# Expert up products with the rows held and the weights moving, GELU before the turn, and row loads issued ahead of the stores

## What is computed

```
logits = h2 @ gate_w + gate_b
wts, sel = top_k(logits, 2);  wts = softmax(wts)
for e in range(8):
    he = gelu(h2 @ w1[e] + b1[e], approximate=False)      # 192 -> 768
    res = res + cw[:, e:e + 1] * (he @ w2[e] + b2[e])     # 768 -> 192
```

## Time and profile before

| | before |
|---|---|
| median of 3 runs | 1596.52 us (1596.47 to 1605.81) |
| the profiled execution | 1584.23 us, its span 1582.5 us |
| mean granted TensorE clock in it | 0.816 |
| stage of the 39 tiles: first up product to last down product | 762.2 to 969.7 us |
| PE, VectorE, ScalarE busy in the span | 79%, 49%, 30% |

### The profile page before, as it was taken

One profiled execution on the slowest core, in us unless ns is written; L12 is line 12 of the kernel. 1 busy time (PEld: TensorE's weight loads), 2 busy tenths in 40 slices (PEclk: granted clock), 3 DMA queues, 4 the chain that ended last, 5 costly groups with the idle time before them and its releaser, 6 DMA issues.

```text
span 1582.5 us, 44760 instructions
## 1 busy us (share of the span) xinstructions
PE 1256.1 (79%) x19426; PEld 978.1 (62%) x19426; DVE 774.9 (49%) x2068; ACT 471.5 (30%) x1022; POOL 238.7 (15%) x248
## 2 busy tenths in 40 slices
PE   5999999987999999973799995174888989875151
PEld 2666666664767777762577773174788888864131
DVE  2133333334555634344233333552577777755876
ACT  1233333323433433233233331042133333223040
POOL 3100000143100000007100003505333333000000
PEclk8599999988988969555799998585888879855565
DMA  9000000213100000013111111100000000000001
GB/s 317 11 22 22 22 22 22 66 47 90 47 2 2 2 2 2 2 46 111 46 36 40 38 38 50 51 0 2 3 4 4 4 3 4 4 2 1 0 0 40
DMA packets 28797, 48.47 MB, mean 31 GB/s; under 512 B 3632, under 2 KB 21696, under 8 KB 28352
## 3 DMA queue, kind: packets, MB, share of 16 engines
q1 hardware_dynamic: 25536, 39.33, 8.1%
q0 software_dynamic: 3072, 6.30, 1.3%
HBM read 33.20 MB, written 12.41 MB: 29 GB/s over the span
## 4 chain that ended last, share of the span: by engine, by line
PE 64%; DVE 17%; POOL 11%; ACT 5%; issue 3%; DMA 1%; POOLq 0%; ACTq 0%; DVEq 0%
PE ps L1023 9%; PE ps L719 8%; PE ps L1135 6%; PE ps L847 4%; PE ps L1038 4%; PE ps L784 3%; POOL big L655 3%; PE ps L725 3%; POOL big L659 3%; PE ps L872 2%; PE ps L909 2%; PE ps L739 2%; POOL rows_dram L634 2%; PE ps L767 2%; PE ps L1183 2%
## 5 line engine op out<-in xcount | busy, mean ns | idle before, releaser
L1135 PE MATMUL ps<-big 128*128 128x32 bf16 x7680 | 217.8, 181 | 52.4 <-DVE big L1918 25.4
L1135 PEld LDWEIGHTS ps<-big 128*128 128x128 bf16 x7680 | 207.2, 99 | 63.8 <-DVE big L1918 29.6
L719 PE MATMUL ps<-big,consts 97*96 97x512 f32 (+1 forms) x256 | 136.3, 660 | 13.7 <-DVE consts L1544 13.7
L1023 PE MATMUL ps<-big 128*128 128x128 bf16 x1170 | 142.0, 219 | 1.1 <-DVE big L1834 0.5
L1023 PEld LDWEIGHTS ps<-big 128*128 x1170 | 112.0, 96 | 27.6 <-issue 2.9
L1841 DVE TENSOR_TENSOR big<-big 128x512 bf16<-128x512 f32 x78 | 41.5, 558 | 104.5 <-ACT big L1448 104.2
L1906 DVE TENSOR_REDUCE big<-ps 128x24 f32<-128x48 f32 x160 | 32.8, 205 | 116.7 <-PE ps L1135 115.7
L1447 ACT ACTIVATE big<-ps 128x512 bf16<-128x512 f32 x78 | 38.2, 490 | 163.6 <-issue 129.8
L719 PEld LDWEIGHTS ps<-big,consts 97*96 97x96 f32 (+1 forms) x256 | 39.7, 174 | 69.3 <-issue 61.8
L655 POOL TENSOR_SCALAR_AFFINE_SELECT big<-big 128x1536 f32<-128x1536 f32 (+1 forms) x32 | 48.7, 1547 | 222.0 <-ACT big L1485 222.0
L1662 DVE TENSOR_REDUCE big<-ps 128x12 bf16<-128x1536 f32 x32 | 56.2, 1758 | 50.8 <-PE ps L872 50.8
(11 more groups left out here) (357 smaller groups left out, 2267.4 us busy)
## 6 DMA issues: line engine op xcount, KB each, us to landing
big<-x_dram SPq DMA_DIRECT2D x16, 384.0 KB, 3.3
consts<-packed_dram SPq DMA_DIRECT2D x1, 4459.0 KB, 17.7
rows_dram<-big SPq DMA_DIRECT2D x1, 3744.0 KB, 17.7
big<-rows_dram SPq DMA_DIRECT2D x39, 96.0 KB, 2.0
results_dram<-big SPq DMA_DIRECT2D x39, 96.0 KB, 1.6
big<-w_dram SPq DMA_DIRECT2D x12, 288.0 KB, 3.6
big<-w_dram SPq DMA_DIRECT2D x16, 192.0 KB, 4.0
big<-w_dram SPq DMA_DIRECT2D x4, 576.0 KB, 5.6
```

Source lines behind the costliest of these rows:

```text
L719: last = nc.tensor.matmul(o[0:HC, :], w[tk_rows(c), c, at:at + HC], xT[tk_rows(c), c, :], start=(c == 0), stop=(c == 1))
L1023: last = nc.tensor.matmul(ps[0][:, 2 * (i % 2) + m // 4, m % 4 * P:(m % 4 + 1) * P], e_at(expert, at, P), side, start=(k == 0), stop=(k == ...
L1135: last = nc.tensor.matmul(sums_wide(g, k), kernel_part(i, part)[:, at:at + P], x, start=(part == 0), stop=(part == 1), skip_group_check=True)
```

## The change

The up products are turned round. The turned rows are now held, and the expert's weights move: 512 columns for the first half of the hidden values, 256 for the second, each half the sum of five products. The hidden values so come out with a row to a partition. One set of PSUM banks (`m_hidden`) takes them instead of two. ScalarE passes each half through GELU once, to f32 (`e_he`). Then PE turns them with six f32 transposes (`m_turn_hidden`) into two banks of PSUM (`m_turned_hidden`), ScalarE copies those to bf16 (`m_hi`), and VectorE subtracts that copy from the PSUM (`m_lo`). The down products are the same, but come a step later. The turned rows move to the two banks of PSUM that became free (`m_x_out`). The load of tile i + 4 is issued ahead of the store of tile i. Two new semaphores take up old ones, and so bear their names in lists: `m_hturned` is `gate_xturned`, `m_hi` is `gate_xn`. In the changed program's list of instructions ScalarE loads a function table once ahead of the first GELU and none between GELU and copy.

```diff
+        M_HALVES = (slice(0, 4 * P), slice(4 * P, HIDDEN))
+        def m_hidden(half):
+            return ps[0][:, half, 0:(4 - 2 * half) * P]
+        def m_x_out(i):
+            return ps[0][:, 2 + i % 2, 0:ROW // 2].bitcast(BF16)
+        def m_turned_hidden(half):
+            return ps[1][:, half, 0:(4 - 2 * half) * P]
...
             for i in range(TILES):
+                if i + 4 < TILES:
+                    load_rows(i + 4)
                 sp.wait_ge(sem("m_y"), i + 1)
                 sp.dma_start(ys[i * P:(i + 1) * P, :], e_y[i % 4]).then_inc(sem(f"m_stored{i % 4}"), 16)
-                if i + 4 < TILES:
-                    load_rows(i + 4)
...
             def m_up(i, expert):
                 pe.wait_ge(sem("m_x"), i + 1)
-                if i >= 2:
-                    pe.wait_ge(sem("m_gelu"), 2 * (i - 1))
                 x = e_x[i % 2]
                 sides = (x[:, 0:P], x[:, P:2 * P], x[:, 2 * P:3 * P], x[:, 0:P], e_xe[i % 2])
-                for m in range(HT):
+                for half, cols in enumerate(M_HALVES):
+                    if i >= 1:
+                        pe.wait_ge(sem("m_gelu"), 2 * (i - 1) + half + 1)
                     for k, side in enumerate(sides):
-                        at = k * HIDDEN + m * P
-                        last = nc.tensor.matmul(ps[0][:, 2 * (i % 2) + m // 4, m % 4 * P:(m % 4 + 1) * P],
-                                                e_at(expert, at, P), side, start=(k == 0), stop=(k == CHUNKS - 1))
-                    if m in (3, 5):
-                        last.then_inc(sem("m_up"), 1)
+                        last = nc.tensor.matmul(m_hidden(half), side,
+                                                e_at(expert, k * HIDDEN + cols.start, cols.stop - cols.start),
+                                                start=(k == 0), stop=(k == CHUNKS - 1))
+                    last.then_inc(sem("m_up"), 1)
+
+            def m_turn_hidden(i):
+                for half, cols in enumerate(M_HALVES):
+                    pe.wait_ge(sem("m_gelu"), 2 * i + half + 1)
+                    if i >= 1:
+                        pe.wait_ge(sem("m_lo"), 2 * (i - 1) + half + 1)
+                    for at in range(cols.start, cols.stop, P):
+                        last = nc.tensor.transpose(m_turned_hidden(half)[:, at - cols.start:at - cols.start + P],
+                                                   e_he[i % 2][:, at:at + P], ident[:, :])
+                    last.then_inc(sem("m_hturned"), 1)
...
-            for i in range(-1, TILES):
-                older = expert
+            for i in range(-1, TILES + 1):
                 if i + 1 < TILES:
-                    expert = pe.value_load(tile_e[0:1, i + 1:i + 2], min_val=0, max_val=EXPERTS - 1)
+                    experts[i + 1] = pe.value_load(tile_e[0:1, i + 1:i + 2], min_val=0, max_val=EXPERTS - 1)
                 if 0 <= i and i + 2 < TILES:
                     m_turn(i + 2)
                 if i + 1 < TILES:
-                    m_up(i + 1, expert)
-                if 0 <= i:
-                    m_down(i, older)
+                    m_up(i + 1, experts[i + 1])
+                if 0 <= i < TILES:
+                    m_turn_hidden(i)
+                if 1 <= i:
+                    m_down(i - 1, experts.pop(i - 1))
...
             def m_gelu(i):
                 if i >= 2:
+                    act.wait_ge(*after("m_hturned", 2 * (i - 1)))
+                for half, cols in enumerate(M_HALVES):
+                    act.wait_ge(sem("m_up"), 2 * i + half + 1)
+                    nc.scalar.activation(e_he[i % 2][:, cols], m_hidden(half), ACT.Gelu).then_inc(sem("m_gelu"), 1)
+
+            def m_hi(i):
+                if i >= 2:
                     act.wait_ge(sem("m_down"), i - 1)
...
+                    act.wait_ge(*after("m_hturned", 2 * i + half + 1))
                     if i >= 2:
                         act.wait_ge(sem("m_lo"), 2 * (i - 2) + half + 1)
...
+                    nc.scalar.activation(e_hi[i % 2][:, cols], m_turned_hidden(half), ACT.Copy).then_inc(sem("m_hi"), 1)
+
+            for i in range(-1, TILES):
+                if i + 1 < TILES:
+                    m_gelu(i + 1)
+                if 0 <= i:
+                    m_hi(i)
...
-                    dve.wait_ge(sem("m_gelu"), 2 * i + half + 1)
-                    nc.vector.tensor_tensor(e_lo[i % 2][:, cols], e_he[i % 2][:, cols], e_hi[i % 2][:, cols],
+                    dve.wait_ge(*after("m_hi", 2 * i + half + 1))
+                    nc.vector.tensor_tensor(e_lo[i % 2][:, cols], m_turned_hidden(half), e_hi[i % 2][:, cols],
                                             ALU.subtract).then_inc(sem("m_lo"), 1)
...
-            for i in range(-1, TILES):
-                if 0 <= i and i + 2 < TILES:
+            for i in range(TILES + 1):
+                if i + 2 < TILES:
                     m_x(i + 2)
-                if 0 < i:
+                if 1 <= i:
                     m_y(i - 1)
-                if i + 1 < TILES:
-                    m_lo(i + 1)
-            m_y(TILES - 1)
+                if i < TILES:
+                    m_lo(i)
```

More of the change, by code:

```diff
@@ L66 @@
     "a_zero": "tk_pv",
+    "m_hi": "gate_xn",
+    "m_hturned": "gate_xturned",
     "t_exp": "tk_on",
@@ L1008, in m_turn @@
                     pe.wait_ge(sem("m_x"), i - 1)
-                o = ps[1][:, i % 2, 0:ROW // 2].bitcast(BF16)
                 for c in range(3):
-                    last = nc.tensor.transpose(o[:, c * P:(c + 1) * P], e_row[i % 4][:, c * P:(c + 1) * P], identb[:, :])
+                    last = nc.tensor.transpose(m_x_out(i)[:, c * P:(c + 1) * P], e_row[i % 4][:, c * P:(c + 1) * P],
+                                               identb[:, :])
                 last.then_inc(sem("m_turned"), 1)
@@ L1049, in _ @@
             m_turn(1)
-            expert = older = None
-            for i in range(-1, TILES):
-                older = expert
+            experts = {}
+            for i in range(-1, TILES + 1):
                 if i + 1 < TILES:
-                    expert = pe.value_load(tile_e[0:1, i + 1:i + 2], min_val=0, max_val=EXPERTS - 1)
+                    experts[i + 1] = pe.value_load(tile_e[0:1, i + 1:i + 2], min_val=0, max_val=EXPERTS - 1)
                 if 0 <= i and i + 2 < TILES:
@@ L1440, in m_gelu @@
                 if i >= 2:
+                    act.wait_ge(*after("m_hturned", 2 * (i - 1)))
[4 more added lines that the diff above has]
+                if i >= 2:
                     act.wait_ge(sem("m_down"), i - 1)
-                for half, cols in enumerate((slice(0, 4 * P), slice(4 * P, HIDDEN))):
-                    act.wait_ge(sem("m_up"), 2 * i + half + 1)
+                for half, cols in enumerate(M_HALVES):
+                    act.wait_ge(*after("m_hturned", 2 * i + half + 1))
                     if i >= 2:
                         act.wait_ge(sem("m_lo"), 2 * (i - 2) + half + 1)
[L1446 to L1451, removed]
+                    nc.scalar.activation(e_hi[i % 2][:, cols], m_turned_hidden(half), ACT.Copy).then_inc(sem("m_hi"), 1)
[4 more added lines that the diff above has]
+                    m_hi(i)
             def a_xT_out(k):
@@ L1831, in m_x @@
                     dve.wait_ge(sem("m_up"), 2 * (i - 1))
-                rows = ps[1][:, i % 2, 0:ROW // 2].bitcast(BF16)
+                rows = m_x_out(i)
                 nc.vector.tensor_copy(e_x[i % 2], rows)
```

## The result

| | before | changed |
|---|---|---|
| median of the runs beside it | 1601.16 us (first shown: 1596.52) | 1541.72 us (1538.96 to 1557.16, 4 runs) |
| ratio to before, 95% interval | | 0.9666 [0.9606, 0.9725] |
| both once more, beside the mixture below | 1593.97 us | 1540.72 us, 0.9699 [0.9637, 0.976] |
| profiled execution: span | 1582.5 us | 1541.4 us |
| first up weight load to last down product | 762.2 to 969.9, 207.7 us | 771.4 to 928.7, 157.3 us |

What follows compares the result with a forecast made beforehand. PE's own work was taken to bound the stage; 39 tiles x 4.01 + 7.0 us for the ends = 163.4 against 207.7, gain 44, so 1552 us. Range 1540 (p, us a tile, 3.9, less 8 us spread) to 1578 (p = 4.7).

Steps and rivals of the forecast that it cites:

- What bounded the kernel: In the stage of up and down products, PE's own work: 5.31 us a tile, up products held by register-address issue.
- Up products, 1.66 us: On PE per tile: five wide products at 0.217 us and five narrow at 0.115, 1.66 us against 3.72.
- Issue and ScalarE: Per tile, both hidden behind PE: 16 register instructions in place of 35, 2.0 us; ScalarE 1.7 us of 4.0.
- Hidden turns, 0.71 us: On PE per tile: six f32 transposes at 0.109 us, 0.65, plus 0.06 for the change from bf16 products.
- The tile, 4.01 us: PE's sum per tile: row turns 0.17, up products 1.66, hidden turns 0.71, down products 1.47; 1.30 less than 5.31.
- The cold start, 4.0 us lost: Start of the stage, 8.1 us at half clock: PE does what takes 4.1 at full clock, 4.0 us lost.
- The drain, 3.0 us lost: End of the stage: the last two tiles have no up products to cover 1.5 us over m_y and m_lo.
- VectorE's margin, 0.3 us: In the loop: m_y and m_lo take 1.5 us from down products to PE, hidden behind 1.83 us of PE work.
- The loads' margin, 0.8 us: Row loads per tile: issued some 1.2 us in, landing after 2.0, at 3.2 of 4.0 us; 0.8 to spare.
- Rival 2: Up products: ten weight loads of 0.097 us not hidden, 4.98 us a tile, gain 7 us, 1590 us; chance 0.04.
- Rival 3: Clock falls in the stage: half-clock tile about 7.8 us; all tiles 1700 us, one dip 1564; chance 0.06.
- From the profile to the median: Whole kernel: the stage's gain of 44 us, profiled span 1538, was carried over to the median, giving 1552 us.

Runs made afterwards that it cites:

- the mixture below: Changed kernel with the last 256 hidden columns back to held weights, subtraction ahead of the sum, loads one store earlier: 1544.41 us, ratio 0.9667 to the kernel before.

## Why the prediction was right, point by point

- *What bounded the kernel.* Right. With the register taken away the old products fell from 124 to 56 ns, near the 54 that the column price gave. The price of one address is 113 ns; the forecast took 115, a mean.
- *Up products, 1.66 us.* Measured 1.62. The narrow ones cost their columns, 109 ns, and not the 115 of issue, since their addresses are made while the wide ones run.
- *Issue and ScalarE.* Right that both hide, with two slips that cost nothing: the kernel before has 36 register instructions a tile (30 and 6), not 35, and the GELU of one tile begins 2.6 us ahead of the next up products (844.99 to 847.56), not a whole tile; it is done 0.87 us after its start.
- *Hidden turns, 0.71 us.* Measured 0.65. The 0.06 for the changeover from bf16 products, which no row had shown, is not there.
- *The tile, 4.01 us.* Measured 3.92. Over 39 tiles that is 3.5 us of the 6.1 by which the stage came out shorter than the 163.4 forecast.
- *The cold start, 4.0 us lost.* Mis-sized. The forecast carried over the 8 us at half clock of the earlier trace rows. In the changed kernel the clock was full 2.1 us into the stage, and 4.6 in the second profile of it, so 1 to 2 us were lost (an estimate, half of that time). This is the rest of those 6.1 us, nearly.
- *The drain, 3.0 us lost.* Right: two waits of 1.34 and 1.43 us at the end, and 2.7 us back when the order was turned.
- *VectorE's margin, 0.3 us.* Right: 0.27. In the tile shown the sum starts 0.2 us behind the down products, as priced.
- *The loads' margin, 0.8 us.* Right for the median: the load issued at 844.63 lands at about 846.6, the turns come at 847.39. Late landings do reach through it: the next load's issue took 1.25 us in place of 0.43, its rows landed 2.9 us after its start, and that one tile took 4.09 us. That undoing the reordering costs in every tile is shown, and it costs more than was worked out, since the clock was lower too.
- *Rival 2, weight loads in the open.* Out. The wide products' spacing had no room for it (ten in 1.62 us), and 30 held weight blocks went at 56 ns a product. The sentence of the Trainium skill on which it stood ("TensorE: Matmul & The Clock Gate", Part 3, "The mechanism") is not what full-height loads do here. The same section of the Trainium skill also lets a load into the background weight buffer go ahead of running products; no run here shows which buffer a load took.
- *Rival 3, the clock.* It stayed at 1.00 from 2.1 us into the stage on (4.6 in the second profile). In the kernel with late loads, where PE waited some 3 us in every tile, it was 0.79 in the mean: there the concern came true.
- *From the profile to the median.* The gain of 44 us was made for the stage and carried over to the median. The stage gained 50.4; the profiled span 41.1, for the attention before it; the ratio of the runs says 53. A span compared with a span would have put the mechanism 9 us too low. The 1552 us were 10 too many. The stage explains 6.1 of them, the tile and the cold start both priced too high; the rest lies within the spread of the runs. The mechanism was right, but that 1541.72 lies inside the range, by 2 us, is in part luck: the lower end came from p = 3.9 and the spread of the executions, with the cold start still at 4 us.

## What to carry to other kernels

Ask of each product what it waits for by holding its price against the clock and against its columns: one that costs the same at half clock is not held by the array; here it was waiting for issue. Where an address stands in a register, make one address serve as many columns as a bank holds, or hide the addresses behind wide products; here the form with held weights was the cheaper one in the stage as soon as issue was hidden. When a pipeline gets one step deeper, look for every transfer that stands in a queue behind the late end of it.

## What was not expected of the hardware

- Products of 128 columns with a register address of their own started 112 to 113 ns apart at the median, whichever side had the address (on the held side at half clock too), and 56 ns apart with fixed ones (30 in 1.67 us).
- f32 transposes of 128 x 128 ran 109 ns apart right behind bf16 products, with the clock at 1.00.
- Loads of 96 KB that landed in 2.0 us at the median landed in up to 4.0 us at times, and single issues on SP took up to 1.66 us in place of 0.43 (1.25 in the changed kernel); in the two kernels with one step more of lead no tile waited for them.
- In the cold start the clock rose 2.1 to 5.0 us after the stage began in the changed kernel and in the experiments, 8.1 us in the kernel before. Why was not tried.
